# Second layer of an MLP's first phase as seven block products for eight, with the block sums spread over VectorE and GpSimd

## Chip, core and metric

One core of a Trainium2 chip runs the whole kernel. The metric is the device time of one execution in microseconds, the median over runs.

## What is computed

The reference, cut to what matters (B = 8 sequences of 256 rows, V = 512, H = 2048, float32):

```
attn_out  = softmax(q k^T / sqrt(V)) v @ Wp + bp
cms_out   = gelu(attn_out @ cW1 + cb1) @ cW2 + cb2
cms_out  += one_hot(target_codes, V)
modifier  = gelu(concat([attn_out, cms_out]) @ mW1 + mb1) @ mW2 + mb2
out       = clip(x + cms_out + modifier, 0, 1)
# then, with the weights of each sequence's expert e:
h         = gelu(out @ W_down[e] + b_down[e]) @ W_up[e] + b_up[e]
result    = layernorm(out + h) * ln_w[e] + ln_b[e]
```

The change is in `gelu(attn_out @ cW1 + cb1) @ cW2`, the second of these two products.

## The kernel before

**Numbers.** Every matrix product is made of three matmuls: each operand is split into a high part (ScalarE copies it to the type fp32r, `act_copy`, L579) and a low part (VectorE subtracts the high part from the operand, `sub`, L1023), and `mm3` (L219 to L222) adds high by low, high by high and low by high into one PSUM bank. A matmul has 128 rows of contraction, 128 output features and 512 token columns.

**Stages.** The 2048 tokens are worked in two batches of 1024, that is of two halves of TB = 512. For each batch `b`: attention, then the MLP (`pe_mlp`, L478), then the expert's layers, which are mixed into the next batch's attention or stand at the end. The MLP has three phases of NQ = 8 quads each: phase 0 is the conditioning MLP (`cW1`, `cW2`), phase 1 the half of `mW1` that meets `attn_out`, phase 2 the half that meets `cms_out`, with `mW2`. A quad is 256 hidden features by 1024 tokens.

**First layer.** The first layer of a quad is a product of 2 x 2 blocks done with seven block products (Winograd's form of Strassen's scheme): weight blocks A11, A12, A22 and the sums S1 to S4 (`dve_s`, L1035, on VectorE, four subtractions or additions of 256 elements), input blocks B11, B21, B22 and the sums T1 to T4, made once per phase. A block product is 2 x 3 = 6 matmuls. The four results, 11, 12, 22 and 21, are gathered in the tile `sbc` (three slots, one quad each) by ScalarE (`act_s`, L631) and VectorE (`dve_c`, L1096), and go through gelu (`act_gelu`, L656).

**Second layer in phases 0 and 2.** ScalarE (`act_hid`, L672) and VectorE (`dve_hid`, L1106) split the four gelu tiles of a quad into high and low parts, 512 elements each, and (`act_w2`, L613, `dve_w2`, L1068) the two rows of second-layer weights that belong to it, 1024 elements. `l2` (L532) makes eight blocks of 6 matmuls per quad: block k is output tile j = k % 4 of token half t = k // 4. Each goes into bank 6 or 7 in turn and is added into `acc` by VectorE (`dve_evac`, L1114, the add at L1129), or for the first quad of a batch written there by ScalarE with the bias (`act_evac`, L639).

**What sets the order.** Each engine's program is an order written out by hand, with semaphores between engines. In `pe_mlp` step `it` has, for it = 2 to 25, the places 1, 2, 7, 5, 6, 4, 3: at each one first-layer block (`first` of quad `it`, or `second` of quad `it - 1`), and after it one second-layer block of quad `it - 2`:

```
                for step, which in enumerate((1, 2, 7, 5, 6, 4, 3)):
                    ...
                    if dn:
                        l2(it - 2, step)
                if dn:
                    l2(it - 2, 7)
```

A block of `l2` waits until the bank it writes has been evacuated (`evac`), the first and the fifth until the tiles they read are split. ScalarE follows `act_mlp` (L840), VectorE `dve_mlp` (L1489) with `dve_mlp_flat` (L1420) for the steps of phase 1. GpSimd has no part in the MLP: `pool_program` (L1612) makes a constant matrix and later some reciprocal square roots (L1625). SyncE issues the loads (`sync_mlp`, L1677; `load_w1` and `load_w2`, 512 KB each) and, in phases 1 and 2, moves partial sums of phase 1 out to `pre_d` and back.

Memory is one arena cut by hand. The split hidden tiles and second-layer weights of phase 0 lie in the region Y0, those of phase 2 in X0; `xf`, the transposed input that the residual needs, stays in the region R0 through phase 0 for the first batch, and is stored to `xt_d` and reloaded (at step 4) for the second.

## Time and profile before

| what | value |
|---|---|
| median of 3 runs | 1053.17 us (1050.83 to 1053.75) |
| profiled execution, its own time | 1052.44 us |
| its span, first to last instruction | 1050.7 us |
| TensorE matmul busy | 1037.3 us, 99% |
| VectorE busy | 788.7 us, 75% |
| ScalarE busy | 527.4 us, 50% |
| GpSimd busy | 7.5 us, 1% |
| matmuls recorded | 4889 |
| mean granted TensorE clock | 0.998 |

The profile is of one execution. In its rows PE is TensorE's matmul side and PEld its weight loads, DVE is VectorE, ACT ScalarE, POOL GpSimd, SP SyncE. An L number is a line of the kernel. Buffer numbers are left out of tile names, and some tiles share a name: `w_lo<-w_raw` is the low part of a weight of either layer, told apart by its size (256 elements for a first-layer block, 1024 for a second-layer pair). Busy time counts the stretches in which at least one instruction of an engine runs, so overlapping matmuls count once. A row of a timeline gives start, duration and, in brackets, the idle time before it and what ended it. The distance between two starts is what one instruction takes of its engine when the engine does not wait; its duration is longer.

### The profile page before, as it was taken

Reading aid. Unit: us, or ns where it says so; the run is one execution under the profiler, and the core shown is the slowest. Engines: PE = TensorE matmul, PEld = TensorE weight load, DVE = VectorE, ACT = ScalarE, POOL = GpSimd, SP = SyncE. Lnnn points to the kernel's source line nnn. Section 1 sums busy time; section 2 is a strip of 40 time slices with the busy share of each in tenths; the row PEclk is TensorE's granted clock in tenths of the full one; section 3 lists DMA queues with packets and bytes.
Section 4 is the critical chain, followed back from the end, with each engine's and each line's share of the span. In section 5 each row is a group of like instructions: output and inputs, shape, how many; then the busy total and the mean of one; then the engine's idle time right before and its main releaser. Section 6 shows DMA issues by size and latency. Waiting matters only on the chain. (4 is left out here: it accounts for less than half of the span.)

```text
span 1050.7 us, 13850 instructions
## 1 busy us (share of the span) xinstructions
PE 1037.3 (99%) x4889; PEld 862.9 (82%) x4889; DVE 788.7 (75%) x1372; ACT 527.4 (50%) x963; POOL 7.5 (1%) x18
## 2 busy tenths in 40 slices
PE   9999999999999999999999999999999999999997
PEld 7889878888888778878889887888888887888886
DVE  5436967776598889887856796777757889887798
ACT  4426875444355444433564487554435644334357
POOL 0000000000000000000000000000000000000001
PEclk9999999999999999999999999999999999999999
DMA  6700221210133363430634222312004322423152
GB/s 165 278 1 21 65 77 41 75 46 21 61 141 120 101 158 123 119 122 41 220 114 117 73 81 80 121 41 79 22 21 160 141 82 99 153 103 106 41 161 80
DMA packets 75165, 101.60 MB, mean 97 GB/s; under 512 B 19966, under 2 KB 54874, under 8 KB 71258
## 3 DMA queue, kind: packets, MB, share of 16 engines
q1 hardware_dynamic: 75008, 100.71, 28.8%
q8 instruction: 39, 0.64, 0.2%
q14 instruction: 28, 0.23, 0.1%
q10 hardware_dynamic: 90, 0.02, 0.0%
HBM read 79.74 MB, written 20.97 MB: 96 GB/s over the span
## 5 line engine op out<-in xcount | busy, mean ns | idle before, releaser
L220 PE MATMUL bank<-hid_hi,w_lo 128*128 128x512 f32 x512 | 201.4, 393 | 3.3 <-DVE acc L1129 2.0
L670 ACT ACTIVATE sbc<-sbc,bias 128x512 f32<-128x512 f32 x112 | 80.9, 724 | 242.3 <-DVE sbc L1104 178.0
L222 PE MATMUL bank<-hid_lo,w_hi 128*128 128x512 f32 x512 | 199.4, 389 | 0.0
L221 PE MATMUL bank<-hid_hi,w_hi 128*128 128x512 f32 x512 | 199.3, 389 | 0.0
L1129 DVE TENSOR_TENSOR acc<-bank,acc 128x512 f32<-128x512 f32 x224 | 153.8, 687 | 50.1 <-PE bank L222 49.5
L220 PE MATMUL bank<-ta_hi,w_lo 128*128 128x512 f32 x448 | 174.8, 390 | 0.0
L222 PE MATMUL bank<-ta_lo,w_hi 128*128 128x512 f32 x448 | 174.3, 389 | 0.0
L221 PE MATMUL bank<-ta_hi,w_hi 128*128 128x512 f32 x448 | 174.3, 389 | 0.0
L1104 DVE TENSOR_TENSOR sbc<-bank,sbc 128x512 f32<-128x512 f32 x144 | 98.2, 686 | 38.3 <-PE bank L222 38.0
L580 ACT ACTIVATE sbc<-bank 128x512 f32<-128x512 f32 x112 | 66.2, 593 | 112.6 <-PE bank L222 112.4
L220 PEld LDWEIGHTS bank<-hid_hi,w_lo 128*128 128x128 f32 x512 | 96.1, 188 | 30.8 <-DVE acc L1129 7.2
L1023 DVE TENSOR_TENSOR w_lo<-w_raw,w_hi 128x256 fp32r<-128x256 f32 (+1 forms) x176 | 93.8, 563 | 36.6 <-ACT w_hi L580 36.6
L222 PEld LDWEIGHTS bank<-hid_lo,w_hi 128*128 128x128 f32 x512 | 96.1, 188 | 20.2
L221 PEld LDWEIGHTS bank<-hid_hi,w_hi 128*128 128x128 f32 x512 | 96.1, 188 | 19.2
L220 PEld LDWEIGHTS bank<-ta_hi,w_lo 128*128 128x128 f32 x448 | 84.1, 188 | 18.9 <-issue 1.6
L222 PEld LDWEIGHTS bank<-ta_lo,w_hi 128*128 128x128 f32 x448 | 84.1, 188 | 17.6
L221 PEld LDWEIGHTS bank<-ta_hi,w_hi 128*128 128x128 f32 x448 | 84.1, 188 | 17.2
L1023 DVE TENSOR_TENSOR hid_lo<-sbc,hid_hi 128x512 fp32r<-128x512 f32 x128 | 87.6, 684 | 12.4 <-ACT hid_hi L580 12.4
L580 ACT ACTIVATE w_hi<-w_raw 128x256 fp32r<-128x256 f32 (+1 forms) x176 | 87.1, 523 | 4.4 <-PE bank L222 4.1
L220 PE MATMUL bank<-tc_hi,w_lo 128*128 128x512 f32 x224 | 87.7, 392 | 0.1
L222 PE MATMUL bank<-tc_lo,w_hi 128*128 128x512 f32 x224 | 87.2, 389 | 0.0
L221 PE MATMUL bank<-tc_hi,w_hi 128*128 128x512 f32 x224 | 87.2, 389 | 0.0
(227 smaller groups left out, 1540.7 us busy)
## 6 DMA issues: line engine op xcount, KB each, us to landing
w_raw<-in_L_cond_mW SPq DMA_DIRECT2D x48, 512.0 KB, 3.4
w_raw<-in_L_cond_cW SPq DMA_DIRECT2D x32, 512.0 KB, 4.3
pre_d<-sbc SPq DMA_DIRECT2D x10, 1024.0 KB, 3.9
sbc<-pre_d SPq DMA_DIRECT2D x10, 1024.0 KB, 7.2
e_raw<-in_L_cond_W_down SPq DMA_DIRECT2D x8, 512.0 KB, 4.6
e_raw<-in_L_cond_W_up SPq DMA_DIRECT2D x8, 512.0 KB, 4.3
out<-acc SPq DMA_DIRECT2D x16, 256.0 KB, 2.1
x_raw<-in_x SPq DMA_DIRECT2D x2, 1024.0 KB, 5.2
```

Source lines behind the costliest of these rows:

```text
L220: nc.tensor.matmul(dst, w_l, a_h, start=start, stop=False, **kw)
L221: nc.tensor.matmul(dst, w_h, a_h, start=False, stop=False, **kw)
L222: return nc.tensor.matmul(dst, w_h, a_l, start=False, stop=stop, **kw)
L580: return nc.scalar.activation(dst, src, ACT.Copy)
L670: nc.scalar.activation(dst, dst, ACT.Gelu, **kw).then_inc(g_done[key], 1)
L1023: sub = lambda dst, a, hi: nc.vector.tensor_tensor(dst, a, hi.bitcast(F32), ALU.subtract)
L1104: nc.vector.tensor_tensor(dst, ps[BANKS[i % 2][bank]][:, :], dst, ALU.add).then_inc(done, 1)
L1129: nc.vector.tensor_tensor(dst, bank[:, :], dst, ALU.add).then_inc(evac, 1)
```

## The change

Phase 0's second layer is put into the same seven-product form. Its 2 x 2 x 2 blocks: contraction over a pair of quads (2 x 256 hidden features), outputs in two halves of 128 features for a fixed m (output tiles m and m + 2), tokens in two halves of 512. A pair of quads needs it twice, for m = 0 and m = 1, so there is one run of seven blocks per quad, called a chain; chain c has m = c % 2 and belongs to pair c // 2. Per quad TensorE makes 7 blocks of 6 matmuls for 8.

What the engines do for it in phase 0:

- **TensorE**: `chain(it - 3, step)` stands at each place of steps 3 to 10, where `l2(it - 2, step)` stood in steps 2 to 9, with the eighth block gone. The order of the blocks is B11, T1, T2, B22, T3, B21, T4. Blocks 1, 2 and 6 of a chain start their bank anew, the other four add to what their bank holds, and after every block the bank is added into `acc`.
- **Input blocks**, once per pair: B11, B22, B21 are pairs of gelu tiles, T1 to T4 sums of them. T1 and T3 are made on GpSimd (`pool_block_sum`), T2 and T4 on VectorE (`dve_block_sum`), each 1024 elements. All seven are split, ScalarE high and VectorE low, 1024 elements each (`act_block`, `dve_block`), in place of the four tiles of 512 per quad. For even chains five blocks are split in the step itself (T2, B22, T3, B21, T4), for the next pair two (B11, T1) in the odd step before.
- **Weight blocks**, per chain: S1 to S4 of 256 elements on GpSimd (`pool_w2_sums`), then seven blocks split in three parts of 256, 1024 and 512 elements (`act_wf`, `dve_wf`). The sums of first-layer weights stay on VectorE.
- **Evacuation**: seven a chain (`dve_chain_evac`), of which ScalarE takes four in chains 0 and 1 (`act_evac`).
- **SyncE**: second-layer weights are loaded by pairs, at steps 4, 6 and 8; `xf` is stored to `xt_d` before the MLP in the first batch too, and reloaded in both at step 11 (the split weights use its place). The T blocks of phase 2 and the residual are made one step later.
- Some semaphores are merged (`bu_in` and `bd_in`, `wp_h` and `wtr_hi` and others).

The diff, cut to its core:

```diff
+            def chain(c, s):
+                p, u = c // 2, 7 * c + s
+                if s in (0, 1, 5):
+                    pe.wait_ge(w2_l, W2B * b + 3 * c + (1, 2, 0, 0, 0, 3)[s])
+                if c % 2 == 0:
+                    pe.wait_ge(f_l, 7 * pair_of(b, p) + s + 1)
+                if u >= 2:
+                    pe.wait_ge(evac, L2B * b + u - 1)
...
+                w, t = WF_NO[F_W[s]], T_NO[F_ORDER[s]]
+                for k in range(2):
+                    last = mm3(ps[6 + u % 2][:, :], wf_hi[:, w, k, :], wf_lo[:, w, k, :], tc_hi[:, t, k, :],
+                               tc_lo[:, t, k, :], s in (0, 1, 5) and k == 0, k == 1, skip_group_check=True)
+                last.then_inc(l2_mm, 1)
...
-                new, old, dn = it < QB, 2 <= it - 1 < QB, has_l2(it - 2)
+                new, old, dn = it < QB, 2 <= it - 1 < QB, it - 2 >= 2 * NQ
...
+                    if 0 <= it - 3 < NQ:
+                        chain(it - 3, step)
...
+        def dve_mlp_low(dve, b, it):
+            c = it - 3
+            heavy, light = c % 2 == 0, c % 2 == 1 and c + 1 < NQ
+            p = c // 2 if heavy else (c + 1) // 2
...
+            if c >= 1:
+                dve_chain_evac(dve, b, c - 1, 6)
+            if heavy:
+                dve_block_sum(dve, b, p, "T2")
+                dve_block_sum(dve, b, p, "T4")
+            dve_w1_second(dve, b, it)
...
+            if heavy:
+                dve_block(dve, b, p, "T2")
+            evac_of(0)
+            dve_c(dve, b, it, "11")
+            evac_of(1)
+            if heavy:
+                dve_block(dve, b, p, "B22")
+            if light:
+                dve_block(dve, b, p, "B11")
+            if c >= 0:
+                dve_wf(dve, b, c, 2)
+            dve_s(dve, b, it + 1)
...
+            evac_of(2)
+            if heavy:
+                dve_block(dve, b, p, "T3")
+            dve_w1_first(dve, b, it + 1, (0, 1))
+            evac_of(3)
+            if heavy:
+                dve_block(dve, b, p, "B21")
+            if light:
+                dve_block(dve, b, p, "T1")
+            evac_of(4)
+            dve_w1_first(dve, b, it + 1, (2,))
+            if heavy:
+                dve_block(dve, b, p, "T4")
+            if c + 1 < NQ:
+                dve_wf(dve, b, c + 1, 0)
+            evac_of(5)
+            if it != 2:
+                dve_c(dve, b, it - 1, "12")
+            if c + 1 < NQ:
+                dve_wf(dve, b, c + 1, 1)
...
+        def pool_w2_sums(pool, b, c):
...
+            if c:
+                pool.wait_ge(l2_mm, chain_no(b, c - 1) + 5)
...
+            nc.gpsimd.tensor_tensor(s1, a21, a22, ALU.add).then_inc(w2_s, 1)
+            nc.gpsimd.tensor_tensor(s3, a11, a21, ALU.subtract).then_inc(w2_s, 1)
+            pool.wait_ge(w2_s, n + 1)
+            nc.gpsimd.tensor_tensor(s2, s1, a11, ALU.subtract).then_inc(w2_s, 1)
+            pool.wait_ge(w2_s, n + 3)
+            nc.gpsimd.tensor_tensor(s4, a12, s2, ALU.subtract).then_inc(w2_s, 1)
+
+        def pool_mlp_low(pool, b):
+            for it in range(2, NQ + 3):
+                c = it - 3
+                if c % 2 and c + 1 < NQ:
+                    pool_block_sum(pool, b, (c + 1) // 2, "T1")
+                elif c % 2 == 0:
+                    pool_block_sum(pool, b, c // 2, "T3")
+                if c + 1 < NQ:
+                    pool_w2_sums(pool, b, c + 1)
```

ScalarE's order in these steps (`act_mlp_low`) is: w1 second part, T2, first copy from a bank, weight part 2 of the chain, w1 first part, B22, gelu 11, T3 (or B11 in odd steps), gelu 22, w1 sums, a copy from a bank, T1 or B21, a copy, T4, weight part 0 of the next chain, gelu 21, weight part 1 (which waits for GpSimd's four sums), gelu 12.

How the instructions stand on two engines. First VectorE, in the middle of phase 0, where one quad ends and the next begins. Before (`L1129` evacuates a block of the second layer, `hid_lo` is the low part of a gelu tile, `s_f` the first-layer sums):

```order
L1104 TENSOR_TENSOR sbc<-bank,sbc 128x512 [waits p3_mm,s2_done]
L1023 TENSOR_TENSOR hid_lo_55<-sbc,hid_hi_53 128x512 [waits hid_h21]
L1129 TENSOR_TENSOR acc<-bank,acc 128x512 [waits evac,l2_mm] x2
L1023 TENSOR_TENSOR hid_lo_55<-sbc,hid_hi_53 128x512 [waits hid_h12]
L1023 TENSOR_TENSOR w_lo_63<-w_raw,w_hi_61 128x256 [waits w1_h2]
L1023 TENSOR_TENSOR w_lo_63<-s_f,w_hi_61 128x512 [waits w1_h2]
L1043 TENSOR_TENSOR s_f<-w_raw 128x256 [waits w1_in1,w1_l2,w1_l1]
```

Now, at the head of an even chain step (`L1276` evacuates, `L1289` is the sum T2 and then T4, `tc_lo` the low part of an input block, `wf_lo` that of second-layer weights, `wf_s` their sums):

```order
L1243 TENSOR_TENSOR sbc<-bank,sbc 128x512 [waits p3_mm,s2_done]
L1162 TENSOR_TENSOR wf_lo<-wf_s,wf_hi 128x1024 [waits w2_h]
L1276 TENSOR_TENSOR acc<-bank,acc 128x512 [waits evac,l2_mm]
L1289 TENSOR_TENSOR tx_f<-sbc,t_f 128x1024 [waits g22_done,t_pool,g12_done,l2_mm]
L1289 TENSOR_TENSOR tx_f<-sbc,tx_f 128x1024 [waits c21_done,t_dve,g11_done,l2_mm]
L1162 TENSOR_TENSOR w_lo_64<-w_raw,w_hi_62 128x256 [waits w1_h2]
L1162 TENSOR_TENSOR w_lo_64<-s_f,w_hi_62 128x512 [waits w1_h2]
L1162 TENSOR_TENSOR tc_lo<-tx_f,tc_hi 128x1024 [waits t_dve,f_h]
L1276 TENSOR_TENSOR acc<-bank,acc 128x512 [waits evac,l2_mm]
```

Between the last sum of a quad's first layer and the next evacuation but one now stand the two block sums and the first block's low part, all of 1024 elements, where two splits of 512 stood.

Then GpSimd. Before, it has nothing between the constant matrix and the square roots. Now it has this for every step of phase 0, here from an even step to the next even step (`tx_f` is T3, `t_f` T1):

```order
L1845 TENSOR_TENSOR tx_f<-sbc 128x1024 [waits proj_out,g22_done,g12_done,c21_done,g11_done]
L1860 TENSOR_TENSOR wf_s<-w_raw 128x256 [waits l2_mm,w2_in1,w2_in0]
L1861 TENSOR_TENSOR wf_s<-w_raw 128x256
L1863 TENSOR_TENSOR wf_s<-wf_s,w_raw 128x256 [waits w2_s]
L1865 TENSOR_TENSOR wf_s<-w_raw,wf_s 128x256 [waits w2_s]
L1840 TENSOR_TENSOR t_f<-sbc 128x1024 [waits g22_done,f_l,g12_done,t_dve,c21_done,g11_done]
```

T3 waits for the same gelus as VectorE's T2; the four weight sums wait for five blocks of the chain before and for both loads.

## Rows read from the trace of the kernel before

**Rows 1.** The page: busy us, share of the span and instructions; granted clock by slice
```profile
PE 1037.3 (99%) x4889; PEld 862.9 (82%) x4889; DVE 788.7 (75%) x1372; ACT 527.4 (50%) x963; POOL 7.5 (1%) x18
...
PEclk9999999999999999999999999999999999999999
```

**Rows 2.** TensorE in order of time: start us, us, engine, line, operation, tiles
```profile
133.65 0.40 PE L220 MATMUL bank<-hid_hi,w_lo 128*128 128x512 f32 x1
133.89 0.40 PE L221 MATMUL bank<-hid_hi,w_hi 128*128 128x512 f32 x1
134.12 0.39 PE L222 MATMUL bank<-hid_lo,w_hi 128*128 128x512 f32 x1
```

**Rows 3.** VectorE in order of time, one step of the first phase [idle before <-releaser]
```profile
179.57 0.69 DVE L1129 TENSOR_TENSOR acc<-bank,acc 128x512 f32<-128x512 f32 x1 [0.62 <-PE bank L222]
...
184.26 0.68 DVE L1023 TENSOR_TENSOR hid_lo<-sbc,hid_hi 128x512 fp32r<-128x512 f32 x1
184.86 0.42 DVE L1023 TENSOR_TENSOR w_lo<-w_raw,w_hi 128x256 fp32r<-128x256 f32 x1
185.20 0.68 DVE L1023 TENSOR_TENSOR w_lo<-s_f,w_hi 128x512 fp32r<-128x512 f32 x1
185.97 0.43 DVE L1043 TENSOR_TENSOR s_f<-w_raw 128x256 f32<-128x256 f32 x1
...
187.44 0.68 DVE L1129 TENSOR_TENSOR acc<-bank,acc 128x512 f32<-128x512 f32 x1
...
197.53 1.23 DVE L1023 TENSOR_TENSOR w_lo<-w_raw,w_hi 128x1024 fp32r<-128x1024 f32 x1 [2.30 <-ACT w_hi L580]
198.67 0.68 DVE L1129 TENSOR_TENSOR acc<-bank,acc 128x512 f32<-128x512 f32 x1
199.97 0.69 DVE L1129 TENSOR_TENSOR acc<-bank,acc 128x512 f32<-128x512 f32 x1 [0.62 <-PE bank L222]
```

**Rows 4.** Windows: us, busy us (instructions) of each engine, clock, DMA
```profile
core 0: us, PE busy (x) PEld busy (x) DVE busy (x) ACT busy (x) POOL busy (x), PEclk, DMA share, GB/s
...
124.80:288.00 163.20, 162.92 (x715) 133.52 (x715) 110.44 (x191) 82.18 (x151) 0.00 (x0) 1.00 0.15 52
288.00:297.60 9.60, 9.60 (x44) 7.96 (x43) 7.56 (x14) 5.76 (x11) 0.00 (x0) 1.00 0.27 96
```

**Rows 5.** Waits, from 126 to 300 us: us in total, times, longest
```profile
ACT sbc L670 <- DVE sbc L1104: 37.2, 19, 3.5
...
DVE acc L1129 <- PE bank L222: 17.8, 23, 2.0
...
PEld bank L220 <- DVE acc L1129: 0.9, 2, 0.6
...
PE bank L220 <- DVE acc L1129: 0.2, 1, 0.2
```

**Rows 6.** ScalarE in order of time, the same step
```profile
191.96 0.72 ACT L670 ACTIVATE sbc<-sbc,bias 128x512 f32<-128x512 f32 x1 [1.96 <-DVE sbc L1104]
...
195.95 0.60 ACT L580 ACTIVATE sbc<-bank 128x512 f32<-128x512 f32 x1 [2.11 <-PE bank L222]
196.44 1.05 ACT L580 ACTIVATE w_hi<-w_raw 128x1024 fp32r<-128x1024 f32 x1
```

**Rows 7.** GpSimd by line and shape: count, busy us, mean ns
```profile
L1625 POOL TENSOR_TENSOR rstd<-veps,mhalf 128x2 f32<-128x2 f32 x5 | 3.5, 696 | 1030.3 <-DVE veps L1251 1030.3
L1625 POOL TENSOR_TENSOR rstd<-veps,mhalf 128x1 f32<-128x1 f32 x6 | 3.2, 544 | 8.0 <-DVE veps L1273 8.0
L1616 POOL TENSOR_SCALAR_AFFINE_SELECT ident<-ident 128x128 f32<-128x128 f32 x1 | 0.3, 292 | 0.2 <-POOL feat_i L1614 0.2
```

**Rows 8.** DMA issues of the run: count, KB each, median us to landing
```profile
w_raw<-in_L_cond_cW SPq DMA_DIRECT2D x32, 512.0 KB, 4.3
...
xt_d<-xf SPq DMA_DIRECT2D x2, 1024.0 KB, 6.1
...
xf<-xt_d SPq DMA_DIRECT2D x2, 1024.0 KB, 7.7
```

More of the change, by code:

```diff
@@ L208, in build @@
         l2_of = lambda b, i: RB * b + (i if i < NQ else i - NQ)
+        L2B, W2B = 7 * NQ + 8 * NQ, 3 * NQ + NQ
+        l2_no = lambda b, i: L2B * b + 7 * NQ + 8 * (i - 2 * NQ)
+        w2_no = lambda b, i: W2B * b + 3 * NQ + (i - 2 * NQ)
+        hid_no = lambda b, i: NQ * b + (i - 2 * NQ)
+        chain_no = lambda b, c: L2B * b + 7 * c
+        F_ORDER = ("B11", "T1", "T2", "B22", "T3", "B21", "T4")
+        F_NO = {n: k for k, n in enumerate(F_ORDER)}
+        F_W = ("A11", "S1", "S2", "S4", "S3", "A12", "A22")
+        WF_NO = {n: k for k, n in enumerate(("A11", "S1", "S2", "S3", "S4", "A12", "A22"))}
+        F_OUT = ((0, 0), (2, 1), (0, 1), (0, 1), (2, 1), (0, 0), (2, 0))
+        pair_of = lambda b, p: NQ // 2 * b + p
         T_ORDER = ("B11", "B21", "T1", "B22", "T2", "T3", "T4")
@@ L627, in act_slot_free @@
                 act.wait_ge(pre_out[j % 3], 16 * pre_count(b, j))
-            else:
-                act.wait_ge(hid_l[key], l2_of(b, j) + 1)
+                return
+            n = pair_of(b, j // 2)
+            if key in ("11", "21"):
+                act.wait_ge(f_l, 7 * n + F_NO["B21" if j % 2 else "B11"] + 1)
+                if j % 2:
+                    act.wait_ge(t_dve, 2 * n + 2)
+                else:
+                    act.wait_ge(t_pool, 2 * n + 1)
+            else:
+                act.wait_ge(t_pool, 2 * n + 2)
+                if j % 2:
+                    act.wait_ge(t_dve, 2 * n + 1)
+                    act.wait_ge(f_l, 7 * n + F_NO["B22"] + 1)
         def act_s(act, b, i, which):
@@ L882, in act_mlp @@
                     act_w1_first(act, b, it + 1, 1)
-                if it == 2:
-                    act_gelu(act, b, it - 1, "21")
-                down(4)
-                down(5)
-                if old and pph != 1 and not border:
+                if old and pph == 2 and not border:
                     act_w2(act, b, it - 1)
@@ L1533, in dve_mlp @@
                     dve_x_lo(dve, 2 * b + 2, (0,))
-                if old and it != 2:
+                if old:
                     dve_c(dve, b, it - 1, "22")
@@ L1581, in dve_mlp @@
                 down(5)
-                if old and it != 2:
+                if old:
                     dve_c(dve, b, it - 1, "12")
@@ L1681, in sync_mlp @@
                     load_w1(sp, b, it + 2)
-                if has_l2(it):
+                if it in range(4, NQ + 2, 2):
+                    sp.wait_ge(w2_l, W2B * b + 3 * (it - 2))
+                    load_w2(sp, b, it - 2)
+                    load_w2(sp, b, it - 1)
+                if has_l2(it) and not 2 <= it < NQ:
                     r = l2_of(b, it)
```

404 lines of the change are left out of this document (283 added, 121 removed).

## The prediction

> **What bounds the kernel now.** I read the busy line first: TensorE has a matmul in flight for 99% of the span, at full granted clock throughout (2.4 GHz, the upper of its two levels); VectorE is busy 75%, ScalarE 50%, GpSimd 1% [rows 1]. A busy TensorE is not a TensorE at its peak, so the next thing is what one matmul takes. The group's mean is about 390 ns, but in the timeline matmuls start every 0.23 us: they overlap, and the spacing is what a removed one gives back [rows 2]. The best figure for it is the period of a whole step of the first phase. The same evacuation on VectorE comes at 179.57 and at 199.97 us, 20.40 us apart [rows 3], and one step is 15 blocks of 6 matmuls, so 20.40 / 90 = 0.2267 us each. Eight such steps fill 124.8 to 288.0 us (163.2 = 8 x 20.40), with TensorE busy in 162.9 us of them; the steps of the second phase, 7 blocks long, follow at 9.52 us (42 x 0.2267; the window shows 9.6) [rows 4]. In that stretch TensorE waits 1.1 us in all for VectorE, against 37.2 us on ScalarE for VectorE and 17.8 us on VectorE for TensorE in one group each [rows 5]. So this stage is bound by TensorE, with VectorE busy 13.8 us in each 20.4 us step (110.44 / 8) and ScalarE 10.3.
>
> Times count from the start of a step on TensorE; a block is 6 x 0.2267 = 1.36 us and a place in the interleaving (a first-layer block and a second-layer block) 2.72 us.
>
> **TensorE.** Eight second-layer blocks a step become seven. 8 steps x 2 batches x 6 matmuls = 96 matmuls, x 0.2267 = **21.8 us less**, if nothing waits. An interleaved step becomes 84 x 0.2267 = 19.04 us. The second layer also starts one step later (step 3) and ends in step 10, which swaps one short step from after to before and costs nothing on TensorE: a short step is 9.52 us at either end. Per batch from step 2: before 8 x 20.40 + 9.52 = 172.7, after 9.52 + 8 x 19.04 = 161.8 us.
>
> **VectorE.** Its steps, start to start, when it does not wait: 0.60 us for 512 elements, 0.34 for 256, 1.14 for 1024, 1.47 for the four sums of a first-layer weight [rows 3]. Before, a step holds 17, 7 and 1 of these sizes, which is 2.4 + 10.2 + 1.1 = 13.7 us, as measured. Now it differs by parity. An even chain step (c = 0, 2, 4, 6) has the sums T2 and T4 and the low parts of T2, B22, T3, B21, T4, all of 1024 elements, the low parts of seven weight blocks (256, 1024, 512), seven evacuations for eight, and no split of the hidden tiles: 8 x 0.34 + 13 x 0.60 + 8 x 1.14 = **19.6 us in a 19.04 us step**. An odd one has two such blocks: 13.9 us. Over a pair that is 33.5 of 38.1 us, so VectorE is not the bound in the mean. But TensorE has two banks for the second layer and takes the blocks in a fixed order, so an even step must be paid for when it comes. Laid out along its instruction order:
>
> - The last block of the step before leaves its first-layer bank at -1.36. VectorE adds it (-1.3 to -0.7), makes the low part of the four weight sums (to 0.45), evacuates the chain's last block (1.05), sums T2 (2.2), waits for its end and sums T4 (3.4), splits w1 (0.34 + 0.60 + a gap, 1.11 in the rows: 4.55), T2 low (5.7), evacuation, c11, evacuation (7.5), B22 low (8.65), weight part 2 (9.25), four w1 sums (10.7), c22, evacuation (11.9), **T3 low, done at 13.05**.
> - TensorE wants T2 at 6.8 (2 places and a block) and has it, with the evacuation of the first block due then too, at 6.3. It wants T3 at 4 x 2.72 + 1.36 = **12.24**, and waits 0.8 us. B21 and T4 then come at 15.5 and 17.9 for 15.8 and 18.5: no further wait.
> - ScalarE makes each high part ahead of this (1.05 us for 1024, 0.72 a gelu, 0.6 a 512 copy [rows 6]): its even step sums to 14.4 us. T3's high part stands before the gelu that waits for c22, so it is not late. But the gelu of the last tile stands behind the high part of the weight sums; where that comes later, the head of the chain moves by up to 0.8 us.
>
> The wait of an even step is thus 0.8 to 1.7 us; I take 1.3, because a dozen handovers of about 0.1 us are in none of these figures. **8 even steps x 1.3 = 10.4 us given back.** Step 2, now only 9.52 us long on TensorE, carries on ScalarE 10.7 us (w1 parts 2.4, three copies from banks 1.8, four gelus 2.9, two blocks 2.1, two weight parts 1.5); its cover was a 20.4 us step. So 1 us a batch more: **2 us**.
>
> **GpSimd and the weight loads.** GpSimd does nothing here today. It gets 8 x 2 sums of 1024 elements and 64 of 256. No row has such an instruction. From below, VectorE's own 0.34 and 1.14 us; from above, one affine select of 128 columns in 0.29 us, so 0.58 and 2.3 if all of it grows with length; the power on 2 elements took 0.70 [rows 7]. I take 0.58 and 2.3, the same engine being nearer. The weight sums may start when the fifth block of the chain is done, at 13.6, and end at about 16.2; ScalarE (1.05) and VectorE (1.14) follow by 18.8, and TensorE wants the result at 4.1 of the next step. Hidden, by 4 us. T1 has a step to spare; T3, ready at 2.8, is wanted by ScalarE at about 8. If GpSimd took 0.70 a sum, still hidden.
>
> SyncE's second-layer loads come in pairs, after part 2 of an odd chain step (about 7.5), 4.3 us to landing each [rows 8]: both there at about 15 with two queued, so the sums of that step end at 17.5 and lose 1 of their 4 us of cover. The residual's copy is now stored and reloaded in both batches. The store (2 x 6.1 us) is in front of the first-layer loads of the MLP on SyncE's queue, tens of us before they are due; the reload (2 x 7.7 us) at step 11 stands between two w1 loads, for a residual at step 15, 38 us on [rows 8]. Its cover is those four steps; without it, 1 or 2 us. Nothing is costed. The T blocks of the third phase move by one step into equally short steps; semaphores that were merged, nothing.
>
> **Sum.** -21.8 + 10.4 + 2 = -9.4 us. On the profiled execution's own 1052.4 us (span 1050.7) that is 1043.0; the median of the runs is 1053.2, and goes to **1044 us**.
>
> **The rivals.**
>
> *VectorE covers all of it.* Were the light steps to lend their slack, or the head of the even step to run earlier, the whole 21.8 us stays: 1031 to 1035. Against it: T3's place in the order is fixed, and 13.05 against 12.24 has no row that shortens it. Chance 0.07.
>
> *GpSimd and VectorE hold each other up (the other side).* T3's sum becomes ready with the same gelu as T2's sum on VectorE. If both cannot read SBUF at once and GpSimd is first, T2 starts 2.3 us after 0.45, not at 1.05: 1.7 us later, on the very chain that is already late, and all 1.7 are lost. The weight sums fall among T4 and w1 of even steps and may take 0 to 1 us more. 8 x 1.7 = 13.6, so **1057 us**, up to 1065. The point from which it decides: the change gains nothing when an even step's wait reaches (172.7 - 161.8 - 1) / 4 = 2.5 us, that is with 1.2 us from GpSimd on top of my 1.3. For it: nearly all of VectorE's instructions there but the evacuations have both inputs in SBUF. Against: nothing in the trace; GpSimd's few instructions stand beside none of that kind. Chance 0.30. The Trainium skill has a rule for exactly this (SBUF — State Buffer, Who interferes with whom): a VectorE instruction with two SBUF inputs contends with a GpSimd instruction that reads SBUF, and whichever comes second waits for the whole of the other. By that rule the time is this rival's 1057; the trace before can neither confirm nor refuse it.
>
> *The weight sums come late.* At 1.15 us a sum (4.6 us from 13.6) ScalarE's gelu behind them is 1.1 us late, and T2 with it: 8 x 1.1 = 9 us back, 1053 us. For it, 0.55 us for one element in the power rows [rows 7]; against, 0.29 for 128 elements. Chance 0.10.
>
> *It does not do what it says, or an order clashes that I have not laid out.* The instruction order does have 96 matmul rows fewer, so the first is out; for the second, 0.05, at 1050 to 1065.
>
> **Chances.** My forecast has 0.48. No change means within 0.3%, 1050.0 to 1056.3, about what a measurement of this kernel tells apart. Faster: 0.45 of the forecast, 0.07, 0.02 of GpSimd's rival and 0.01 of the late sums: 0.55. Same: 0.03 + 0.08 + 0.07 + 0.02 = 0.20. Slower: 0.20 + 0.02 + 0.03 = 0.25. The forecast's own range is 1039 (waits of 0.8 us, none at the start) to 1047 (1.7 us); the range reaches down to 1035 and up to 1061, taking in most of the GpSimd case.
>
> **What would show it.** Right: 19.0 us from one odd step to the next and 20.3 for the even; TensorE's wait in even steps before the fifth chain block, on the low part of T3 (line of the split helper), 0.8 to 1.7 us each, and next to none in odd ones; about 96 matmuls fewer. For the GpSimd rival: VectorE's 1024-element sums at the head of an even step taking over 1.2 us, or starting when GpSimd's T3 ends, and TensorE waiting already at the third chain block, on T2 or on the evacuation behind it. For the late sums: ScalarE waiting on GpSimd. Waits of even steps over 2.5 us in the mean would make the prediction wrong in sign; over 2 us of waits in odd steps or in the second phase would make the account wrong, whatever the total.

## The result: 1084.5 us, 3.0% slower

The change takes 1084.53 us (median of 4 runs, 1082.73 to 1085.88), the kernel before 1052.55 us in the runs beside it: a ratio of 1.0304, with a 95% interval of 1.0282 to 1.0327. The forecast was 1044 us with a range up to 1061, and 0.55 on faster. It is wrong in sign and out of range. One of the rivals named the main cause, at less than half of its price.

The page after: busy us, share of the span and instructions, then the granted clock by slice, as in [rows 1].

```profile
PE 1024.7 (95%) x4793; PEld 848.2 (78%) x4793; DVE 872.8 (81%) x1396; ACT 552.6 (51%) x987; POOL 120.5 (11%) x98
...
PEclk9999989999999999999999998999999999999999
```

The 96 matmuls are gone (4889 to 4793) and TensorE's busy time fell, but its share of the span went from 99% to 95%. VectorE is busy 84 us more. The clock line, all nines before, has eights now.

The waits from 126 to 300 us (us in total, times, longest), where [rows 5] stood before:

```profile
ACT sbc L773 <- DVE sbc L1243: 28.8, 11, 6.0
...
ACT wf_hi L611 <- POOL wf_s L1865: 20.1, 7, 3.3
PEld bank L237 <- DVE tc_lo L1162: 13.2, 8, 3.2
...
ACT tc_hi L611 <- DVE tx_f L1289: 9.0, 3, 3.2
PE bank L237 <- DVE acc L1276: 7.7, 4, 2.8
PE bank L237 <- ACT sbc L768: 7.6, 1, 7.6
```

Before, TensorE waited 0.2 us here for VectorE. Now it waits 7.7 us in four waits for evacuations and 7.6 us once for a gelu. Its weight loads, which run beside the matmuls, wait 13.2 us for low parts of input blocks. ScalarE has two waits that had no counterpart: for the weight sums of GpSimd, and for the sums T2 and T4 of VectorE.

**The gap after step 2.** TensorE in order of time, as in [rows 2]:

```profile
130.12 0.39 PE L239 MATMUL bank<-ta_lo,w_hi 128*128 128x512 f32 x1
138.12 0.77 PE L237 MATMUL bank<-ta_hi,w_lo 128*128 128x512 f32 x1 [7.61 <-ACT sbc L768]
138.68 0.63 PE L238 MATMUL bank<-ta_hi,w_hi 128*128 128x512 f32 x1
139.11 0.63 PE L239 MATMUL bank<-ta_lo,w_hi 128*128 128x512 f32 x1
...
141.67 0.47 PE L239 MATMUL bank<-tc_lo,wf_hi 128*128 128x512 f32 x1
141.98 0.40 PE L237 MATMUL bank<-tc_hi,wf_lo 128*128 128x512 f32 x1
142.22 0.40 PE L238 MATMUL bank<-tc_hi,wf_hi 128*128 128x512 f32 x1
```

For 8 us after the matmul at 130.12 no matmul starts. Then they come 0.43 us apart until 141.67 and 0.23 apart from there. The windows (columns as in [rows 4]) put the granted clock beside it:

```profile
core 0: us, PE busy (x) PEld busy (x) DVE busy (x) ACT busy (x) POOL busy (x), PEclk, DMA share, GB/s
...
138.00:142.00 4.00, 3.88 (x10) 3.10 (x11) 3.70 (x4) 2.50 (x4) 2.07 (x1) 0.52 0.00 0
142.00:146.00 4.00, 4.00 (x19) 3.29 (x18) 3.87 (x5) 2.27 (x4) 0.56 (x1) 1.00 0.00 0
```

0.52 is the lower of the two levels. From 138.12 to 141.98 there are 9 intervals in 3.86 us where 0.2267 each would give 2.04: the idle time costs 1.8 us more after its end. The second batch has the same gap (7.5 us at 656.9). ScalarE's order of time shows what TensorE waited for, the gelu of tile 21 of quad 1 that ends at 137.98:

```profile
130.58 0.72 ACT L773 ACTIVATE sbc<-sbc,bias 128x512 f32<-128x512 f32 x1 [2.90 <-DVE sbc L1243]
131.20 1.04 ACT L611 ACTIVATE tc_hi<-sbc 128x1024 fp32r<-128x1024 f32 x1
132.15 0.71 ACT L773 ACTIVATE sbc<-sbc,bias 128x512 f32<-128x512 f32 x1
134.54 0.63 ACT L611 ACTIVATE w_hi<-s_f 128x512 fp32r<-128x512 f32 x1 [1.69 <-DVE s_f L1185]
...
137.29 0.69 ACT L768 ACTIVATE sbc<-bank,bias 128x512 f32<-128x512 f32 x1
```

Step 2 has four first-layer blocks and no second layer, 24 x 0.2267 = 5.4 us (a `second` block comes only from step 3 on, the program's `2 <= it - 1`, also in the kernel before, where the description of the order gave it to step 2 as well); its last matmul starts at 130.12, so its first at about 124.9. The first block of step 3 needs the bank that this gelu reads. ScalarE waits 2.9 us for VectorE until 130.58, and every row shown lies behind the step's end.

A part of that lateness comes from GpSimd. Its sum T1 starts in the middle of the step, together with a low part of 256 elements on VectorE that takes 2.67 us here and 0.42 where nothing runs beside it (in the runs below in which T1 reads nothing the gap is 5.7 us and not 7.6):

```profile
125.52 2.39 POOL L1840 TENSOR_TENSOR t_f<-sbc 128x1024 f32<-128x1024 f32 x1 [123.95 <-ACT sbc L773]
```

```profile
125.53 2.67 DVE L1162 TENSOR_TENSOR w_lo<-w_raw,w_hi 128x256 fp32r<-128x256 f32 x1 [1.18 <-ACT w_hi L611]
```

**The even steps.** Three engines around the head of an even step, first GpSimd's T3, then VectorE, then TensorE:

```profile
183.40 2.65 POOL L1845 TENSOR_TENSOR tx_f<-sbc 128x1024 f32<-128x1024 f32 x1 [2.02 <-ACT sbc L773]
```

```profile
182.56 1.23 DVE L1162 TENSOR_TENSOR wf_lo<-wf_s,wf_hi 128x1024 fp32r<-128x1024 f32 x1 [0.59 <-ACT wf_hi L611]
183.71 3.42 DVE L1289 TENSOR_TENSOR tx_f<-sbc,t_f 128x1024 f32<-128x1024 f32 x1
187.26 1.23 DVE L1289 TENSOR_TENSOR tx_f<-sbc,tx_f 128x1024 f32<-128x1024 f32 x1
...
189.34 1.22 DVE L1162 TENSOR_TENSOR tc_lo<-tx_f,tc_hi 128x1024 fp32r<-128x1024 f32 x1
190.47 0.69 DVE L1276 TENSOR_TENSOR acc<-bank,acc 128x512 f32<-128x512 f32 x1
```

```profile
188.56 0.39 PE L239 MATMUL bank<-ta_lo,w_hi 128*128 128x512 f32 x1
191.31 0.47 PE L237 MATMUL bank<-tc_hi,wf_lo 128*128 128x512 f32 x1 [2.36 <-DVE acc L1276]
```

T2's sum at 183.71 takes 3.42 us. The same form without company takes 1.22 (experiment 2). It ends at 187.13, that is 1.08 us after GpSimd's T3 (183.40 + 2.65 = 186.05), about what the sum takes of its engine (1.14), as if it had stood still until T3 was done. All eight T2 sums of the run, 3.43 to 2.82 us long, end 1.08 us after their T3, however long before they started. Everything behind it on VectorE is 2.2 us later, the evacuation at 190.47 among it, and TensorE waits 2.36 us for that. Four groups of VectorE from 120 to 300 us (count, busy us, mean ns):

```profile
L1276 DVE TENSOR_TENSOR acc<-bank,acc 128x512 f32<-128x512 f32 x44 | 30.0, 682 | 1.2 <-ACT acc L690 0.9 <-PE bank L239 0.2
...
L1162 DVE TENSOR_TENSOR w_lo<-w_raw,w_hi 128x256 fp32r<-128x256 f32 x29 | 18.3, 659 | 1.8 <-ACT w_hi L611 1.8
...
L1289 DVE TENSOR_TENSOR tx_f<-sbc,t_f 128x1024 f32<-128x1024 f32 x4 | 12.5, 3117 | 0.0
...
L1162 DVE TENSOR_TENSOR wf_lo<-w_raw,wf_hi 128x256 fp32r<-128x256 f32 x8 | 7.1, 888 | 0.0
```

The evacuations, with one input in PSUM, are what they were in [rows 3] (0.68). The three with both inputs in SBUF are far over their 0.42 and 1.23. GpSimd by line and form:

```profile
L1861 POOL TENSOR_TENSOR wf_s<-w_raw 128x256 f32<-128x256 f32 x16 | 23.1, 1443 | 0.0
L1845 POOL TENSOR_TENSOR tx_f<-sbc 128x1024 f32<-128x1024 f32 x8 | 21.2, 2646 | 29.1 <-ACT sbc L773 29.1
L1840 POOL TENSOR_TENSOR t_f<-sbc 128x1024 f32<-128x1024 f32 x8 | 20.5, 2560 | 176.9 <-ACT sbc L773 176.9
```

The shortest single ones are 2.39 us for 1024 elements and 0.73 for 256, so the means are stretched too: each holds up the other. Over all 64, a weight sum takes 1.13 us in the mean.

### The profile page after: what moved, and what is told of

It is laid out like the page before. It is cut to its first block and busy times, and to the rows that moved or that the text cites. A ratio compares the mean times of both kernels' runs of the same rounds, so it can differ in the third digit from the quotient of the medians.

```text
span 1080.9 us, 13969 instructions
## 1 busy us (share of the span) xinstructions
PE 1024.7 (95%) x4793; PEld 848.2 (78%) x4793; DVE 872.8 (81%) x1396; ACT 552.6 (51%) x987; POOL 120.5 (11%) x98
## 5 line engine op out<-in xcount | busy, mean ns | idle before, releaser
L237 PE MATMUL bank<-tc_hi,wf_lo 128*128 128x512 f32 x224 | 90.8, 406 | 25.0 <-DVE acc L1276 15.9
L237 PEld LDWEIGHTS bank<-ta_hi,w_lo 128*128 128x128 f32 x448 | 84.9, 189 | 34.7 <-issue 17.1
L237 PE MATMUL bank<-hid_hi,w_lo 128*128 128x512 f32 x256 | 100.7, 393 | 2.6 <-DVE acc L1266 1.4
L239 PE MATMUL bank<-hid_lo,w_hi 128*128 128x512 f32 x256 | 99.7, 389 | 0.0
L238 PE MATMUL bank<-hid_hi,w_hi 128*128 128x512 f32 x256 | 99.7, 389 | 0.0
L1162 DVE TENSOR_TENSOR w_lo<-w_raw,w_hi 128x256 fp32r<-128x256 f32 (+1 forms) x160 | 88.1, 583 | 4.3 <-ACT w_hi L611 4.3
L238 PE MATMUL bank<-tc_hi,wf_hi 128*128 128x512 f32 x224 | 88.8, 397 | 0.0
L239 PE MATMUL bank<-tc_lo,wf_hi 128*128 128x512 f32 x224 | 88.4, 395 | 0.0
L1266 DVE TENSOR_TENSOR acc<-bank,acc 128x512 f32<-128x512 f32 x112 | 76.7, 687 | 14.4 <-PE bank L239 13.8
L611 ACT ACTIVATE w_hi<-s_f 128x512 fp32r<-128x512 f32 x92 | 57.2, 622 | 37.7 <-DVE s_f L1185 37.7
L237 PEld LDWEIGHTS bank<-tc_hi,wf_lo 128*128 128x128 f32 x224 | 43.0, 192 | 42.0 <-DVE tc_lo L1162 27.0
```

The source lines that it names most:

```text
L237: nc.tensor.matmul(dst, w_l, a_h, start=start, stop=False, **kw)
L238: nc.tensor.matmul(dst, w_h, a_h, start=False, stop=False, **kw)
L239: return nc.tensor.matmul(dst, w_h, a_l, start=False, stop=stop, **kw)
L611: return nc.scalar.activation(dst, src, ACT.Copy)
L1162: sub = lambda dst, a, hi: nc.vector.tensor_tensor(dst, a, hi.bitcast(F32), ALU.subtract)
L1266: nc.vector.tensor_tensor(dst, bank[:, :], dst, ALU.add).then_inc(evac, 1)
```

## The experiments

The theories: **A**, GpSimd's reads of SBUF hold up VectorE's instructions with two SBUF inputs; **B**, VectorE's even step is overfull by its own work; **C**, the gap after step 2 is a matter of ScalarE's work in a step of four blocks; and later **D**, GpSimd is too slow by itself.

**1. GpSimd writes, but reads nothing** (the same edit in all six sums):

```diff
-                nc.gpsimd.tensor_tensor(t1_f[:, :, :], sbc[:, 2 * p % 3, 1:3, :], block_raw(p, "B11"), ALU.subtract)\
-                    .then_inc(t_pool, 1)
+                nc.gpsimd.memset(t1_f[:, :, :], 0.5).then_inc(t_pool, 1)
```

> All of GpSimd's block and weight sums in phase 0 become memsets of the same tiles, with the same waits and the same semaphores: the sums are left out, GpSimd only writes and reads nothing. Theory A (GpSimd's reads hold up VectorE's instructions with two SBUF inputs): the stretched ones (3.40 us instead of 1.23 for T2, 2.67 instead of 0.42 at the start of step 2) come back to 1.23 and 0.42, TensorE's wait in even steps falls from 3.5 to 1.3 or 1.7 us, the gap after step 2 from 7.8 to about 4, together 1060 to 1066 us. Theory B (VectorE's even step is overfilled by its own work, GpSimd is incidental): the even waits stay near 3.5 us and the time above 1078. Theory C (the gap after step 2 is ScalarE's own queue of 10.7 us in a step of four blocks, 5.4 us): the gap stays above 5 us whatever GpSimd does.

Measured: 1052.8 us (10 runs), ratio 1.0008 (0.9997 to 1.0020). The loss of 32 us is gone to within 1 us of the kernel before; I had expected 1060 to 1066 us. The runs spread more than others (1050.5 to 1058.1), and the trace is of the slowest. TensorE's waits in steps 4 to 10 are 0.85 us at most (they were up to 2.8), and the gap after step 2 is 5.7 us instead of 7.6, so theory C holds too. What GpSimd costs is thus as much as the whole loss. But the constant writes are also shorter than the sums (0.96 us for 2.4), so this run does not tell A from D.

**2. Writes as long as the sums.**

```diff
+        def pad_set(pool, *tiles):
+            for t in tiles[:-1]:
+                pads[0] += 1
+                nc.gpsimd.memset(t, 0.5).then_inc(pad, 1)
+                pool.wait_ge(pad, pads[0])
+            return nc.gpsimd.memset(tiles[-1], 0.5)
...
-            nc.gpsimd.tensor_tensor(block_raw(p, "T3"), block_raw(p, "B22"), sbc[:, 2 * p % 3, 1:3, :], ALU.subtract)\
-                .then_inc(t_pool, 1)
+            pad_set(pool, block_raw(p, "T3"), block_raw(p, "T3"), tx_f[:, T_NO["T3"], 0, :]).then_inc(t_pool, 1)
```

> The changed kernel with every GpSimd sum replaced by constant writes to the same tile, repeated until they take about as long as the sum does with nothing beside it (three writes, about 2.4 us, for 1024 elements; two, about 0.7 us, for 256). Leaves out the sums T1, T3 and S1 to S4 of the second layer. GpSimd is thus as late as in the change, but reads nothing. If the loss comes from its reads standing in VectorE's way (A): 1052 to 1057 us, as with the short writes (1052.8), and VectorE's sum T2 at 1.2 to 1.5 us. If it comes from GpSimd being slow, so that T3 and the weight sums arrive late (D): 1070 us or more, with ScalarE waiting for GpSimd and then TensorE for ScalarE or VectorE. Both halves: 1062 to 1068.

Measured: 1053.5 us (10 runs), ratio 1.0011 (1.0000 to 1.0022). GpSimd's rows of this run, VectorE's groups in the same window as above, and ScalarE's wait for the weight sums:

```profile
L1837 POOL MEMSET wf_s<- 128x256 f32 x64 | 20.0, 313 | 162.1 <-PE bank L240 161.2
...
L1837 POOL MEMSET tx_f<- 128x1024 f32 x16 | 15.3, 955 | 33.5 <-ACT sbc L774 33.0
...
L1839 POOL MEMSET tx_f<- 128x512 f32 x8 | 4.2, 526 | 0.5
```

```profile
L1277 DVE TENSOR_TENSOR acc<-bank,acc 128x512 f32<-128x512 f32 x48 | 32.8, 684 | 10.4 <-PE bank L240 9.5 <-ACT acc L691 0.9
...
L1163 DVE TENSOR_TENSOR w_lo<-w_raw,w_hi 128x256 fp32r<-128x256 f32 x31 | 12.0, 417 | 1.9 <-ACT w_hi L612 1.9
...
L1290 DVE TENSOR_TENSOR tx_f<-sbc,t_f 128x1024 f32<-128x1024 f32 x4 | 4.9, 1216 | 0.0
...
L1163 DVE TENSOR_TENSOR wf_lo<-w_raw,wf_hi 128x256 fp32r<-128x256 f32 x8 | 3.3, 417 | 0.0
```

```profile
ACT wf_hi L612 <- POOL wf_s L1839: 5.6, 7, 1.1
```

GpSimd needs 2 x 0.96 + 0.53 us for a large block and 2 x 0.31 for a small one, and nothing is later for it. All of VectorE's forms are at their undisturbed length, and T2's sum went from 3117 to 1216 ns. D falls, A stands: with the durations that GpSimd has when nothing runs beside it, its lateness costs under 1 us; its reading costs 31. That price has two ways to arise, and this run takes away both: VectorE's instructions are longer, and so are GpSimd's own. The four weight sums of a chain take 3.6 to 5.3 us in the change and 2.7 here, and ScalarE waits 20.1 us for them there and 5.6 here. In the change the four sums of T2, 29 parts `w_lo` and 8 parts `wf_lo` above are longer by 4 x 1.90 + 29 x 0.24 + 8 x 0.47 = 18.4 us in a batch, and the low parts of input blocks and of `s_f` by another 3.7 (12 of `tc_lo<-tx_f` by 0.18 us each are most of it). 31 us is 15.5 a batch, so a part of these 22 us fell where VectorE had slack. What B has left is the wait for T3's low part, the step that the forecast named:

```profile
229.29 0.50 PE L238 MATMUL bank<-tc_hi,wf_lo 128*128 128x512 f32 x1 [0.85 <-DVE tc_lo L1163]
```

**3. One half at a time.** Constant writes for T1 and T3 alone, then for the weight sums alone.

```diff
-            nc.gpsimd.tensor_tensor(block_raw(p, "T3"), block_raw(p, "B22"), sbc[:, 2 * p % 3, 1:3, :], ALU.subtract)\
-                .then_inc(t_pool, 1)
+            nc.gpsimd.memset(block_raw(p, "T3"), 0.5).then_inc(t_pool, 1)
```

```diff
-            nc.gpsimd.tensor_tensor(s1, a21, a22, ALU.add).then_inc(w2_s, 1)
+            nc.gpsimd.memset(s1, 0.5).then_inc(w2_s, 1)
```

> Only the two large sums a pair, T1 and T3, become constant writes on GpSimd; the small sums of second-layer weights stay real. Leaves out T1 and T3. If the contention is with T3 at the head of even steps, as my rival had it (A1): most of the 32 us comes back, 1055 to 1060 us. If it is as much with the weight sums (A2, by count of elements read: 4 x 2 x 256 x 2 steps a pair against 2 x 2 x 1024, equal): about 1068.

> The other half: the sums of second-layer weights become constant writes, T1 and T3 stay real. Leaves out S1 to S4 of the second layer. A1: 1076 to 1082 us, little comes back. A2: about 1068. If the two gains of this run and of the one before add up to well under 32 us, either half alone makes the even step late; if to well over, they cover one another.

Measured: 1058.6 us (1.0055, 1.0037 to 1.0074) without the reads of T1 and T3, 1070.7 us (1.0171, 1.0154 to 1.0188) without those of the weight sums. The weight sums by themselves thus cost 1058.6 - 1052.8 = 5.8 us, T1 and T3 by themselves 17.9, both 31.7 (by the ratios, each to its own runs of the kernel before, 4.9, 17.1 and 31.1). The first result is in the range of A1; the second is nearer the 1068 of A2 than the 1076 of A1. A2 in its plain form is refused, since equal numbers of elements read have a price of 6 and of 18 us; that the place decides is likely, but no run moves an instruction of one size to another place. 8 to 9 us exist only when both are there. Perhaps a step that is already late has no slack for the second; no run shows it.

**4. One input instead of two.**

```diff
-            nc.gpsimd.tensor_tensor(block_raw(p, "T3"), block_raw(p, "B22"), sbc[:, 2 * p % 3, 1:3, :], ALU.subtract)\
-                .then_inc(t_pool, 1)
+            nc.gpsimd.tensor_copy(block_raw(p, "T3"), block_raw(p, "B22")).then_inc(t_pool, 1)
```

> The changed kernel with every GpSimd sum replaced by a copy of one of its inputs: GpSimd reads one tile of SBUF where it read two, at the same places. Leaves out the sums T1, T3 and S1 to S4 of the second layer. If reading at all is what stands in VectorE's way (A, first form): VectorE's two-input instructions beside a copy are again stretched to about 2 us and the time is 1060 to 1085 us, by how long the copies take (1024 elements: 1 to 2.4 us). If only an instruction with two inputs on both sides does it (A, second form): 1052 to 1054 us, VectorE at 1.23 us for 1024 elements throughout.

Measured: 1058.0 us (1.0054, 1.0037 to 1.0071), between the two ranges. The timelines decide it, GpSimd first, VectorE second:

```profile
125.17 1.04 POOL L1840 COPY t_f<-sbc 128x1024 f32<-128x1024 f32 x1 [123.61 <-ACT sbc L773]
...
137.87 1.31 POOL L1844 COPY tx_f<-sbc 128x1024 f32<-128x1024 f32 x1 [9.51 <-ACT sbc L773]
```

```profile
137.05 1.23 DVE L1162 TENSOR_TENSOR wf_lo<-wf_s,wf_hi 128x1024 fp32r<-128x1024 f32 x1 [0.29 <-ACT wf_hi L611]
138.19 2.06 DVE L1289 TENSOR_TENSOR tx_f<-sbc,t_f 128x1024 f32<-128x1024 f32 x1
140.38 1.23 DVE L1289 TENSOR_TENSOR tx_f<-sbc,tx_f 128x1024 f32<-128x1024 f32 x1
```

T2's sum starts at 138.19 while the copy runs and takes 2.06 us. It ends at 140.25, that is 1.07 us after the copy (139.18); all eight end 1.07 or 1.08 us after theirs. So it is the first form of A: one reading input on GpSimd's side is enough, and the price is what is left of the other's duration. My range assumed longer copies; with 1.0 to 1.3 us for 1024 elements they make the sum 0.25 to 0.85 us longer instead of 1.6 to 2.2.

**5. How far TensorE is from being the bound.** The last block of each chain made twice, 96 matmuls more; the second pass adds the block again, so the output has it doubled.

```diff
-                for k in range(2):
+                for k in range(4 if s == 6 else 2):
```

> The last block of each chain is multiplied twice, so TensorE has its 96 matmuls (21.8 us) back, and everything else is as in the changed kernel (the output tile of that block is doubled). If TensorE were the bound of phase 0 as before, the time would rise by all 21.8 us, to 1106. If VectorE bounds the even steps (A and B alike), a block more there is hidden in the waits and only the odd steps pay: about +11 us, 1095. If it rises by less than 5 us, TensorE is nowhere the bound in phase 0.

Measured: 1092.7 us (1.0387, 1.0369 to 1.0405), 8.1 us over the change, where I had expected about 11. 96 matmuls are 21.8 us at full spacing, so nearly two thirds of the time that they need was idle time.

**6. All sums on VectorE, GpSimd idle.**

```diff
             if heavy:
                 dve_block_sum(dve, b, p, "T2")
                 dve_block_sum(dve, b, p, "T4")
             dve_w1_second(dve, b, it)
+            if heavy:
+                pool_block_sum(dve, b, p, "T3")
+            elif light:
+                pool_block_sum(dve, b, p, "T1")
...
             evac_of(4)
+            if c + 1 < NQ:
+                pool_w2_sums(dve, b, c + 1)
```

> All sums of phase 0 on VectorE, GpSimd idle: T1 or T3 behind the second w1 split, the four weight sums behind the fifth evacuation. VectorE gets 1.14 + 1.47 us more per step: 22.2 us in even steps, 16.5 in odd ones. Theory A: that is less than what GpSimd's reads take from it now (2.2 us at T2 alone, and about 1 us each in three or four other places), so the time falls, to 1066 to 1074 us, with a step pair of about 41.5 us for 43. Theory B: 2.6 us more in each even step, 8 x 2.6 = 21, 1100 us or more.

Measured: 1075.4 us (1.0217, 1.0200 to 1.0234). The work that GpSimd was to take off VectorE costs VectorE less when it makes it itself: 9 us less than in the change. The time is 1.4 us over the range that A had. VectorE still fills the pairs of steps: they come 41.4 us apart in place of 39.3 in experiment 1. VectorE is busy 870.9 us in this run and 872.8 in the change, which was to relieve it.

**7. Step 2 in another order.** First the one gelu that TensorE waited for moved to the head of ScalarE's step 2:

```diff
+            if it == 2:
+                act_gelu(act, b, it - 1, "21")
             act_w1_second(act, b, it)
...
-            if pre:
+            if pre and it != 2:
                 act_gelu(act, b, it - 1, "21")
```

> ScalarE makes the gelu of tile 21 of quad 1, which frees the bank that TensorE waits 7.6 us for after step 2, first in step 2 instead of fifteenth. If that one place in the order is the cause, the gap goes: -15 us, and 4 us of lower clock behind it, 1066. Theory C (the whole queue of step 2 is late): the next things TensorE needs, the low parts of the first weight block (done at 138.8) and of T1 (137.9), are as late as the gelu, and the time stays within 2 us of 1084.

Measured: 1080.6 us (1.0282, 1.0261 to 1.0302), 4 us less, between the 1066 and the 1082 and more that I had given the two theories. The gap became one of 5.2 us for a weight part of VectorE and one of 2.2 us for an evacuation of ScalarE. Then the whole step in another order on both engines (the list of ScalarE):

```diff
+            if it == 2:
+                act_gelu(act, b, 1, "21")
+                act_w1_second(act, b, 2)
+                act_s(act, b, 2, 1)
+                act_w1_first(act, b, 3, 0)
+                act_block(act, b, 0, "B11")
+                act_gelu(act, b, 1, "22")
+                act_gelu(act, b, 1, "12")
+                act_wf(act, b, 0, 0)
+                act_s(act, b, 2, 5)
+                act_block(act, b, 0, "T1")
...
+                return
```

> The whole change, all sums real, with step 2 alone written in another order on ScalarE and VectorE: the gelu of tile 21 of quad 1 first, then that of 22 and 12 before the blocks of the chain and the weight parts. If the gap after step 2 is only a matter of which ScalarE work stands before the bank that TensorE wants (C): the gap of 7.6 us shrinks to 1 to 3 us in both batches and its slow clock goes, 1084.5 - 2 x (5 to 7) = 1070 to 1075 us. If it is the sum of ScalarE's work in a step that is 5.4 us long on TensorE (C'), the wait only moves to the next bank or to the first chain block: 1078 to 1084.

Measured: 1078.1 us (1.0244, 1.0227 to 1.0261), 6.4 us less than the change, at the fast end of what C' gave. The waits around step 2 fall from 7.6 to 0.7 + 2.5 us, but 1.9 us come back as a wait for ScalarE's evacuation in the first chain, and the slow matmuls did not go as I expected: over the whole second layer 29 and 23 intervals in the two batches are about 0.43 us long, where the change has 12 and 13. So both C and C' hold in part: the order gives back 3.2 us a batch, about a third of the gap and the slow matmuls behind it (7.6 + 1.8 us).

**8. Both causes away together** (experiment 1 and the second order of experiment 7).

> Both causes taken away together: the GpSimd sums are constant writes (leaves out T1, T3 and the second-layer weight sums), and step 2 is in the other order on ScalarE and VectorE. With writes alone it was 1052.8 us with a gap of 5.7 us after step 2; the other order alone gave back 6.5 us of 1084.5. If the two add up: 1043 to 1047 us, which is about where my forecast stood, and the sum of the forecast then lacked these two terms and no other. If the slot behind step 2 eats the gain: 1049 to 1053.

Measured: 1048.0 us (ratio 0.9957, 0.9941 to 0.9974), 1 us above my range for the sum of the two and under the other range. With the reads gone and step 2 reordered the seven-product form is faster than eight products, by 4.4 us. It is no usable kernel, since six sums are not computed. TensorE's two waits in the first chain, in the first batch, are what the gap has become:

```profile
135.54 0.50 PE L237 MATMUL bank<-tc_hi,wf_lo 128*128 128x512 f32 x1 [1.10 <-DVE wf_lo L1178]
...
140.86 0.47 PE L237 MATMUL bank<-tc_hi,wf_lo 128*128 128x512 f32 x1 [2.31 <-ACT acc L690]
```

**9. Two versions that compute everything**, both with the other order of step 2: T3 alone moved from GpSimd to VectorE (first diff), and all sums moved there, in step 2 as in the second diff and elsewhere as in experiment 6.

```diff
             dve_w1_second(dve, b, it)
+            if heavy:
+                pool_block_sum(dve, b, p, "T3")
...
-                elif c % 2 == 0:
-                    pool_block_sum(pool, b, c // 2, "T3")
```

```diff
+                dve_c(dve, b, 2, "11")
+                pool_w2_sums(dve, b, 0)
+                dve_wf(dve, b, 0, 0)
+                pool_block_sum(dve, b, 0, "T1")
+                dve_block(dve, b, 0, "T1")
```

> All computed. Step 2 in the other order, and T3, the GpSimd sum that stood beside the head of the even steps, on VectorE behind the first-layer weight of that step (1.14 us more there); T1 and the weight sums stay on GpSimd. From the runs so far: writes for T1 and T3 gave 1058.6, the other order another 6, T3's own 8 x 1.14 us on the late chain costs 9, and T1 on GpSimd perhaps 4: about 1064 us. If T3's time on VectorE is hidden behind other waits, 1055 to 1060; it would have to be under 1050 to beat the kernel before.

> All computed, every sum on VectorE, GpSimd idle, and step 2 in the other order. With the order of the change this was 1075.4 us with a gap of 6.2 us after step 2. The other order puts 3.9 us of sums into VectorE's step 2 as well. If that step is then bound by VectorE: 1070 to 1076. If the order frees it as before: 1065 to 1070. VectorE's work for a pair of steps is 33.5 + 5.0 = 38.5 us against TensorE's 38.1, so no order gives the forecast's 1044.

Measured: 1072.3 us (1.0188, 1.0166 to 1.0210) and 1073.0 us (1.0190, 1.0173 to 1.0207). Neither comes near 1052.6. The first is 8 us over what I expected. Its even steps but the first are 1.1 to 2.7 us longer than those of experiment 3's first kernel, 1.8 in the mean, where T3 takes 1.14 us on VectorE; and I had left out a wait of 3.3 us for a low part in the first chain (at 145.7 us, and again in the second batch), which was not there while the gap was. In the second, TensorE's two waits for VectorE in the first chain are 3.1 and 1.9 us. No version that beats the kernel before was found.

## Why the prediction was wrong

By its own steps:

- **The 96 matmuls and their spacing** were right: 4793 recorded, 0.23 us apart where TensorE does not wait at full clock.
- **GpSimd, "I take 0.58 and 2.3 ... Hidden, by 4 us."** This is the step that failed, and not by the durations: undisturbed they were 0.73 and 2.39 us. Experiment 2 shows that such durations are hidden. Unpriced was what the instructions do to VectorE, and VectorE to them, while they run. It costs 31 us of the 41 between 1044 and 1084.5.
- **The rival "GpSimd and VectorE hold each other up"** had the mechanism, at 1057. It put T2 1.7 us later; measured were 1.90 us on average over four sums. Its size failed in the rest: "the weight sums ... may take 0 to 1 us more". They stretched `w_lo` and `wf_lo` by 10.8 us a batch (29 x 0.24 + 8 x 0.47), odd steps included, and where both kinds meet one late step they cost 8 us more than each alone. The break-even that the forecast gave, 1.2 us from GpSimd in an even step, was passed by T2's sum alone. And 0.30 was a low chance, as the rival's condition stood in nearly every row of VectorE there. The Trainium skill's rule (SBUF — State Buffer, Who interferes with whom) says that the second waits for the whole of the other, that an instruction with at most one SBUF input is not concerned, and that a GpSimd instruction that only writes is not either. The runs agree on all three: 3.42 for 1.22 us, evacuations at 0.68 us throughout, and writes cost nothing in experiment 2.
- **"Step 2, now only 9.52 us long on TensorE ... So 1 us a batch more: 2 us."** The second failure, a plain misreading of the program: step 2 has no `second` blocks and is 5.4 us long, so 10.7 us of ScalarE's work had about half of the cover counted. The same miscount stands in "Eight such steps fill 124.8 to 288.0 us", where step 2 has 12 blocks and not 15; before and after alike, so it drops out of the 21.8 us. Measured without contention (experiments 1 and 2) there is a gap of 5.7 us a batch, 11.3 us in both; with contention 7.6 us, and 1.8 us of lower clock behind it. The clock was in no term at all.
- **VectorE's overfull even steps, "1.3 x 8 = 10.4 us"**: the place was right, the low part of T3, and 0.85 us is in the foretold 0.8 to 1.7. But in experiment 2 the first even step of a batch shows no such wait, the next 0.28 us and two 0.85 us. From one chain to the next the last three even steps take 19.65, 20.21 and 20.25 us where 19.04 would do: 2 x 3.0 = 6.0 us in all for the 10.4. The term was 4 us too large; the other two were too small by far more.
- **The rival "The weight sums come late"** had its condition, 1.15 us a sum, nearly met: 1.13 us, though only because VectorE holds the sums up (0.73 alone). ScalarE waits for them 20.1 us in that window, and VectorE 4.8 us for ScalarE's copy of them. The 9 us were too many: in the first kernel of experiment 3 the sums are as slow (1.09 us, ScalarE waits 19.1 us), and all that they cost there, by being late and by holding VectorE up, is 5 to 6 us. What their lateness adds beside T1 and T3 was not separated.
- **SyncE, the loads, `xf`** at nothing: no wait of TensorE in the two stretches read (110 to 320 and 630 to 850 us) is on a DMA.
- **The third phase** at nothing: this was not so. At its first block TensorE waits 1.18 us in each batch of the change (at 367.77 and 886.98), as long in experiments 2 and 8, and not at all in the kernel before:

```profile
367.77 0.47 PE L237 MATMUL bank<-tc_hi,w_lo 128*128 128x512 f32 x1 [1.18 <-issue]
```

The profile names nothing that it waited for. VectorE's step there has a low part of a T block (1.14 us) that it did not have before, so the move "into equally short steps" is the likely cause; no run tests it.

One slip in the range moves nothing: with waits of 0.8 us and none at the start its own terms give 1053.2 - 21.8 + 6.4 = 1037.8 us, not 1039.

The sum again, now from the traces. Over both batches I add what the intervals between matmul starts exceed 0.2267 us by, wherever one is over 0.30 us, from before the second layer to its last matmul: 2.4 us in the kernel before.

| kernel | excess, us | -21.8 + excess - 2.4 | span against 1050.7 |
|---|---|---|---|
| forecast | 12.4 (on top of before) | -9.4 | |
| the change | 52.0 | +27.8 | +30.2 |
| experiment 2, writes as long as the sums | 23.8 | -0.4 | +0.8 |
| experiment 8, writes and other order | 18.0 | -6.2 | -4.7 |

So the account by TensorE's idle time holds to 1 to 2.4 us in these three, with 96 matmuls at 0.2267 us as forecast. The wait at the third phase adds 2 x 1.34 = 2.7 us to each, which closes the change (30.5 for 30.2) and leaves the other two 1.2 to 1.5 us off, on the other side. Not every run closes so well: the sum without it gives -0.7 for +5.6 in the trace of experiment 1 and +17.9 for +24.4 in that of experiment 6. Part of that is a wait of 2.4 us for an evacuation in the third phase of the first batch (1.2 in the change, 0.9 in the kernel before). The forecast had its losses in the wrong places, and too small.

What stays open: the rest of these differences, in the stretches not counted or in intervals under 0.30 us; and whether some finer placing of GpSimd's sums, beside VectorE's evacuations alone, would bring the change under 1052. That was not tried.

## What to carry to other kernels

Before moving work from VectorE to GpSimd, look at what VectorE does at that time. Where its instructions have both inputs in SBUF and it has little slack, an instruction of GpSimd that reads SBUF can cost VectorE up to what is left of its own duration, which is about twice that of the same work on VectorE (2.39 for 1.22 us): here VectorE was as busy with the sums moved off it (872.8 us) as with all of them on it (870.9). And cost the step that opens a pipeline against the blocks that it issues itself, counted from the conditions in the loop, not against a step of the steady state; a gap there can be paid again in the clock (1.8 us behind 7.6).
